# Transposing the quantised weight tiles by DMA instead of on TensorE, and leaving them byte-interleaved

## The reference

```python
agg_w = jnp.einsum('bk,koi->boi', att, weight[..., 0])
y = jnp.einsum('boi,bih->boh', agg_w, x) + agg_b[:, :, None]
def _bitlinear(x, w):
    scale = jnp.mean(jnp.abs(w))
    q = jnp.round(jnp.clip(w / (scale + EPS), -1.0, 1.0))
    return x @ (q * scale).T
gate, up = _bitlinear(y, w_gate), _bitlinear(y, w_up)      # w_gate, w_up: 2752 x 1024
return x + _bitlinear(gate * up, w_down)                    # w_down: 1024 x 2752
```

## Time and profile before

| | us |
|---|---|
| median of the runs | 1797.23 |
| the profiled execution | 1797.76 |
| its span, first to last instruction | 1796.0 |
| TensorE busy (with ends that are modelled) | 1738.4 |
| VectorE, ScalarE, GpSimd busy | 1118.9, 541.0, 141.4 |
| chunk 0's groups, from the first to the last matmul | 61.0 to 252 |
| chunk 0's downs | 260.2 to 334.7 |

### The profile page before, as it was taken

How to read it: one execution, slowest core, us unless ns; L and a number is a source line. 1 busy time by engine, 2 the same in 40 slices (tenths; PEclk the granted TensorE clock), 3 DMA queues, 4 the chain that set the end, 5 groups by cost and what they waited for, 6 DMA issues and landing times.

```text
span 1796.0 us, 29810 instructions
## 1 busy us (share of the span) xinstructions
PE 1738.4 (97%) x11897; PEld 1165.2 (65%) x11897; DVE 1118.9 (62%) x1831; ACT 541.0 (30%) x845; POOL 141.4 (8%) x96
## 2 busy tenths in 40 slices
PE   5698999999999999999999999999999999999999
PEld 3244454444545959678685968679594977768584
DVE  5989965686442545856467555855468455766464
ACT  4677441122211313323132312323132322333030
POOL 0854510010000000000000000000000000000000
PEclk9799999999999999999999999999999999999999
DMA  8437511243002312242113312141022412222021
GB/s 314 155 128 258 156 53 71 100 183 123 4 24 79 113 40 103 80 158 79 69 56 138 118 42 97 69 173 63 27 98 106 150 62 93 73 101 81 21 104 47
DMA packets 56557, 180.10 MB, mean 100 GB/s; under 512 B 6112, under 2 KB 6432, under 8 KB 56416
## 3 DMA queue, kind: packets, MB, share of 16 engines
q1 hardware_dynamic: 53712, 163.60, 26.1%
q0 software_dynamic: 2480, 14.22, 2.0%
q10 hardware_dynamic: 224, 0.28, 0.0%
HBM read 147.07 MB, written 31.01 MB: 99 GB/s over the span
## 4 chain that ended last, share of the span: by engine, by line
PE 90%; DVE 3%; issue 2%; ACT 1%; POOL 1%; DMA 1%; SPq 0%; DVEq 0%; POOLq 0%; ACTq 0%
PE ps L795 43%; PE ps L609 25%; PE ps L852 20%; PE ps L813 2%; DVE msk L1297 1%; ACT g_r L970 1%; DVE msk L1289 1%; POOL ys L577 1%; DMA bbc<-biasd 1%; PE ps L689 0%; ACT wgT L1005 0%; POOL ab L588 0%; POOL bbc L588 0%; DMA inter<-in_L_cond_b_dram 0%; DVE ys L1216 0%
## 5 line engine op out<-in xcount | busy, mean ns | idle before, releaser
L795 PE MATMUL ps<-yp,wgT 128*128 128x256 f16 x3528 | 773.4, 273 | 1.6 <-DVE xr L1346 1.0
L795 PE MATMUL ps<-wuT,wgT 128*128 128x256 f16 x3528 | 773.4, 273 | 0.0
L795 PEld LDWEIGHTS ps<-yp,wgT 128*128 128x128 fp8e4 x3528 | 345.3, 98 | 44.5 <-issue 3.5
L795 PEld LDWEIGHTS ps<-wuT,wgT 128*128 128x128 fp8e4 x3528 | 345.2, 98 | 41.4
L852 PE MATMUL ps<-wdT,inter 128*128 128x512 fp8e4 x1680 | 371.3, 379 | 0.0
L852 PEld LDWEIGHTS ps<-wdT,inter 128*128 128x128 f16 x1680 | 163.8, 98 | 194.7 <-issue 1.1
L1606 DVE SCALAR_TENSOR_TENSOR xr<-ps,osc,xr 128x512 f32<-128x512 f32 x180 | 134.1, 748 | 146.6 <-PE ps L852 111.5
L1555 DVE TENSOR_TENSOR wdT<-ps,msk 128x512 f32<-128x512 f32 (+1 forms) x66 | 44.0, 666 | 177.9 <-PE ps L795 177.9
L609 PE MATMUL ps<-yp,wgT 128*128 128x512 f16 x672 | 151.8, 384 | 2.9 <-DVE yp L1251 1.8
L609 PE MATMUL ps<-yp,wuT 128*128 128x512 f16 x672 | 152.8, 384 | 0.0
L609 PE MATMUL ps<-wdT,inter 128*128 128x512 fp8e4 x672 | 147.7, 379 | 0.0
(11 more groups left out here) (230 smaller groups left out, 1708.7 us busy)
## 6 DMA issues: line engine op xcount, KB each, us to landing
wgT<-wcomb SPq DMA_DIRECT2D x60, 896.0 KB, 4.7
wdT<-dcomb SPq DMA_DIRECT2D x12, 2240.0 KB, 10.6
xa<-in_x_dram SPq DMA_DIRECT2D x8, 2048.0 KB, 8.0
out_dram<-xr SPq DMA_DIRECT2D x64, 256.0 KB, 2.0
wdT<-in_L_ffn_w_up_dram SPq DMA_DIRECT2D x10, 512.0 KB, 4.7
wcomb<-raw POOLq DMA_DIRECT2D x11, 448.0 KB, 2.7
ys<-in_L_ffn_w_down_dram SPq DMA_DIRECT2D x9, 512.0 KB, 4.4
wcomb<-msk POOLq DMA_DIRECT2D x10, 448.0 KB, 2.7
```

Of the source, the lines that this page charges most:

```text
L795: last = nc.tensor.matmul(out, w, operand(i, OPERAND[what])[:, k, :], start=(start and h + k + i == 0), stop=(k == KQ - 1 and i == 1), ski ...
```

## The change

The four steps keep their places in `order0`, but the transposing is no longer an instruction of TensorE. SyncE issues a transposing DMA per tile, from `msk` (2-byte words, up to four blocks of 128x128) straight into the weight tensors, whose layout changes: the pairs of bytes stay pairs, so that a matmul reads its weights at a step of two bytes (`weight`, `down_weight`). Four semaphores `s_te`, one per `msk` buffer, tell that a tile has landed; TensorE waits for them ahead of a group, and VectorE before it quantises tile n + 4. `copy_T` and `identb` are gone, and so is GpSimd's part of the quantising: VectorE makes both instructions for all 68 tiles. The remainder of 704 columns is quantised in three pieces instead of two. All sums after the gate matrix's are on ScalarE (before, 15 of 46 were on VectorE). The opening is in another order: `agg_w(1, g)` after the norms, its copies on ScalarE, and other places for the first sums. In `combine` the three plain copies go to ScalarE (`copies`), and GpSimd's store waits for both engines.

```diff
-    SUM_DVE = (0, 1, 7, 10, 17, 21)
-    on_act = [i not in SUM_DVE if i < NG else i % 4 != 1 if i < 2 * NG else
-              i % 3 != 1 if i < 2 * NG + 12 else i % 2 == 0 for i in range(NQ)]
+    SUM_DVE = (0, 1, 7, 10, 17, 20)
+    on_act = [i not in SUM_DVE for i in range(NQ)]
...
-        wgT = sb("wgT", [P, KH, FT * P], f8)
...
-        wdT = sb("wdT", [P, FT + 1, H], f8)
+        wgT = sb("wgT", [P, FT, KH * P], f8)
...
+        wdT = sb("wdT", [P, (FT + 1) // 2, 2 * H], f8)
...
+        def weight(w, f, k):
+            return w[:, f, (k % KQ) * 2 * P:(k % KQ + 1) * 2 * P].rearrange("p (c i) -> p i c", i=2)[:, k // KQ, :]
...
+        def transposed(n):
+            if n < 2 * NG:
+                f = hidden(n)
+                if f < FT:
...
+            r, m = divmod(n - 2 * NG, DP)
+            count = -(-tiles[n][2] // (2 * P))
+            return wdT[:, m * KQ:m * KQ + count, :].bitcast(bf16)[:, :, r * P:(r + 1) * P]
+        def transpose_done(n):
+            return s_te[n % NM], 16 * (n // NM + 1)
...
+                last = buf[:, both:both + 2 * P].rearrange("p (c i) -> p i c", i=2)
+                parts.append((src[:, both:both + P], last[:, 0, :]))
+                parts.append((src[:, both + P:cols].unsqueeze(1).broadcast_to([rows, 2, FR]),
+                              last[:, 1, :].rearrange("p (z c) -> p z c", z=2)))
+            return parts
...
+            def transpose(n):
+                rows, cols = tiles[n][1:]
+                sp.wait_ge(s_q, n + 1)
+                width = -(-cols // (2 * P)) * 2 * P
+                sp.dma_start(transposed(n), msk[0:rows, n % NM, 0:width].bitcast(bf16),
+                             transpose=True).then_inc(s_te[n % NM], 16)
...
+                    while turned < NQ and (turned <= n0 if quant else place_s >= NG and
+                                           quant_at[turned] < order0.index(("S", place_s))):
+                        transpose(turned)
+                        turned += 1
...
-            for n in range(1, NQ, 2):
...
-                raw_arrived(pool, q_load[n])
...
-                nc.gpsimd.tensor_scalar(gts[n // 2 % 2][0:rows, 0:cols], raw(q_load[n]),
-                                        thr[0:rows, m:m + 1], None, ALU.is_gt).then_inc(s_gt, 1)
...
-            def transpose(n):
...
-                pe.wait_ge(s_q, n + 1)
-                if n >= 2:
-                    pe.wait_ge(s_te, n - 1)
...
-                buf = msk[0:rows, n % NM, :].bitcast(bf16)
...
-                    w = min(P, width - q)
-                    last = nc.tensor.transpose(bank[0:w, q:q + rows], buf[:, q:q + w], identb[0:rows, 0:rows])
-                last.then_inc(s_t, 1)
...
                 conv(0, k)
-                if k % 2:
-                    agg_w(1, k // 2)
             norms(0)
+            for g in range(OG):
+                agg_w(1, g)
             norms_T(0)
             total(0)
             for what, n in order0:
-                if what == "T" and n != 1:
-                    transpose(n)
-                elif what == "W":
...
                 elif what == "G":
-                    if n == 0:
-                        pe.wait_ge(s_te, 1)
...
-                    pe.wait_ge(s_te, NG + n + 1)
+                    if n == 0:
+                        pe.wait_ge(*transpose_done(FT))
+                    pe.wait_ge(*transpose_done(NG + n))
                     group(0, FT + n)
...
-            for k, n in enumerate((4, 5, 6, 8, 9, 11, 12, 13)):
+            for n in (4, 5, 6, 8, 9):
                 raw_sum(n)
+            for k, n in enumerate((11, 12, 13, 14, 15, 16, 18, 19)):
                 magnitudes(0, k)
-            for n, tiles_y in ((14, ()), (15, ()), (16, (0, 1)), (18, (2, 3)), (19, ()), (20, (4, 5, 6, 7))):
                 raw_sum(n)
-                for k in tiles_y:
-                    hi_y(0, k)
-            copy_T(0)
+            raw_sum(21)
+            for g in range(OG):
+                act.wait_ge(s_agg, OG + g + 1)
+                agg_copy(nc.scalar.copy, 1, g, s_agg1)
+            for k in range(KH):
+                hi_y(0, k)
...
+            def copies(i):
...
+                for b, a, r in ((0, 0, 0), (3, 0, 1), (6, 1, 1)):
+                    last = nc.scalar.copy(blocks7(i)[:, b, :, :], source(i, a, r), saturate=False)
+                last.then_inc(s_combA, 1)
...
-                if n % 2 == 0:
-                    raw_arrived(dve, e)
...
-                    last.then_inc(s_gtv, 1)
-                    dve.wait_ge(s_gtv, n // 2 + 1)
...
-                    if n >= NM:
...
+                if n >= NM:
+                    dve.wait_ge(*transpose_done(n - NM))
+                for src, dst in quantised(n):
+                    last = V.tensor_scalar(dst, src, thr[0:rows, m:m + 1], None, ALU.is_gt, saturate=False)
+                last.then_inc(s_gtv, 1)
+                dve.wait_ge(s_gtv, n + 1)
+                for src, dst in quantised(n):
+                    last = V.scalar_tensor_tensor(dst, src, nthr[0:rows, m:m + 1], dst, ALU.is_lt, ALU.subtract,
                                                   saturate=False)
...
-                if k in (2, 4, 6, 7):
-                    g = (k - 1) // 2
-                    dve.wait_ge(s_agg, OG + g + 1)
-                    agg_copy(1, g)
-                if k in (3, 5):
-                    raw_sum(7 if k == 3 else 10)
+            raw_sum(7)
+            raw_sum(10)
             scales(0)
             for k in range(SCD):
                 scale_y(0, k)
             raw_sum(17)
-            for k in range(4):
+            raw_sum(20)
+            partition_sums(0, NG)
+            for k in range(2):
                 split_y(0, k)
-            raw_sum(21)
-            partition_sums(0, NG)
...
-                for b, src in ((0, b11), (3, b21), (6, b22)):
-                    V.tensor_copy(st[:, b, :, :].bitcast(f16), src.bitcast(f16))
```

More of the change, by code:

```diff
@@ L145, in adaln_ternary_ffn @@
     assert nt == NQ and ns == NQ
+    ends = (NG, 2 * NG, NQ)
+    quant_at = {n: -1 for n in range(NM)}
+    for at, (what, n) in enumerate(order0):
+        if what == "T" and n + NM not in range(ends[min(n // NG, 2)], ends[min(n // NG, 2)] + NM):
+            quant_at[n + NM] = at
+        elif what == "W":
+            quant_at[n * NG] = at
+        elif what == "Q":
+            quant_at[n] = at
+    assert len(quant_at) == NQ
     ctx = ExitStack()
@@ L239, in adaln_ternary_ffn, with agg_copy @@
         attd = inter[:, 4:6, :].rearrange("p h (o b) -> p h o b", b=B // 2)
-        def agg_copy(h, g):
+        def agg_copy(copy, h, g, done):
             half = B // 4
@@ L246, in agg_copy @@
             for e in range(2):
-                nc.vector.tensor_copy(dst[e * C:(e + 1) * C, :, h * half:(h + 1) * half, g],
-                                      src[e * C:(e + 1) * C, :, :, e]).then_inc(s_aggv, 1)
+                copy(dst[e * C:(e + 1) * C, :, h * half:(h + 1) * half, g],
+                     src[e * C:(e + 1) * C, :, :, e]).then_inc(done, 1)
         def bias_row(c):
@@ L356, in adaln_ternary_ffn @@
         s_thr = sem("s_thr")
-        s_gt = sem("s_gt")
         s_gtv = sem("s_gtv")
         s_q = sem("s_q")
-        s_t = sem("s_t")
-        s_te = sem("s_te")
+        s_te = [sem(f"s_te{i}") for i in range(NM)]
         s_x = sem("s_x")
@@ L474, in _ @@
                 sp.dma_start(raw(e), tiles[n][0]).then_inc(s_raw[s], 16)
+            while turned < NQ and quant_at[turned] < order0.index(("U", UP - 3)):
+                transpose(turned)
+                turned += 1
             sp.wait_ge(s_xr, NT)
@@ L478, in _ @@
             load_x(1)
+            while turned < NQ:
+                transpose(turned)
+                turned += 1
             sp.wait_ge(s_q, NQ)
@@ L730, in down @@
                 elif isinstance(c, int) and c == 0:
-                    pe.wait_ge(s_te, NQ)
+                    for w in range(NQ - NM, NQ):
+                        pe.wait_ge(*transpose_done(w))
                 else:
@@ L812, in leftover @@
                 for w, x in ((FT, inter_r[:, rows]), (FT - 1, f_last[0][:, rows]), (FT - 1, f_last[1][:, rows])):
-                    last = nc.tensor.matmul(bank[:, :], x, wdT[:, w, cols], start=(start and w == FT), stop=True,
+                    last = nc.tensor.matmul(bank[:, :], x, down_weight(w, cols), start=(start and w == FT), stop=True,
                                             skip_group_check=True)
@@ L1066, in _ @@
                 hi_y(1, k)
+            def copies(i):
+                if i < 2:
+                    for w in range(NQ - NM, NQ):
+                        act.wait_ge(*transpose_done(w))
+                else:
+                    act.wait_ge(s_wst[i % 2], 16 * (i // 2))
+                for b, a, r in ((0, 0, 0), (3, 0, 1), (6, 1, 1)):
+                    last = nc.scalar.copy(blocks7(i)[:, b, :, :], source(i, a, r), saturate=False)
+                last.then_inc(s_combA, 1)
+            for i in range(DN - 1):
```

(4 more changed lines are left out.)

146 lines of the change are left out of this document (51 added, 95 removed).

## The result

The changed kernel takes 1809.43 us (median of 4 runs, 1807.32 to 1810.34); the kernel before, on the same chip, 1797.31 (1796.82 to 1797.75). The ratio is 1.0064, 95% interval 1.0052 to 1.0076: slower by 12.1 us. The forecast was 1792.

A forecast was written before the change was run, and what follows sets the result against it. Chunk 0 was taken as bound by TensorE's transposes alternating with VectorE's work. Gains of 9.6, then 13.2 us shrink to 7.7 and 4.5, and end at 5.1 off 1797.76: 1792.7, less 0.5 for the median, 1792; range 1784 to 1825.

The forecast's parts named there:

- Part 1: Quantising by VectorE alone: 1.98 us for each of 68 tiles; losing GpSimd's half costs and gives nothing.
- Part 2: Opening: first group ends near 66 instead of 67, worth 1 us (0 to 2); tile 1's quantising starts at 61.3.
- Parts 3 and 4: Chunk 0's gate groups, then up tiles: second threshold at 104.4, 9.6 us gained at tile 22; product 0 at 149.2, 13.2 gained.
- the unknown: The transposing DMA's price in chunk 0: landing taken as 4.4 us, free up to 5.5, so nothing added; 9.0 would add 37.
- rival B: Tiles 1 to 43: the four-buffer ring paces VectorE, or SyncE's issues exceed 1.98 us a tile; typically 1812, chance 0.26.
- Part 5: Product 0 to third threshold: ScalarE's row of sums takes 16.6 us, threshold at 166.0, gain left 7.7.
- Part 6: Product 4 to product 16 of chunk 0: VectorE bounds it, 56.7 us; product 16 at 229.0, gain shrinks to 4.5.
- Part 7: Product 16 to chunk 0's downs: 26.1 us, with waits for the next `x` and bias; downs at 255.1 instead of 260.2.
- Part 8: The rest after chunk 0's downs start: ScalarE's extra combine copies fit under 3.45 us a group, so nothing added.
- rival E: Weights read at a two-byte step slow TensorE's matmuls: 1800 to 1945, chance 0.05.
- C: Third threshold does not wait for ScalarE's row of sums and comes at 160.5, all after it 5.5 earlier: 1786, chance 0.11.
- D: No difference: waits for `x` and bias and the low clock after two idle stretches take 4 us more: 1797, chance 0.14.

The follow-up runs named there:

- e8: The kernel before, with VectorE making both comparisons of every tile and GpSimd none: 1795.61 us, ratio 0.9994.
- e1: The changed kernel, with transposes issued one ahead of each load of two eight-load bursts instead of behind them: 1802.26 us, ratio 1.0027.
- e2: The changed kernel, with six buffers of quantised tiles instead of four: 1802.29 us, ratio 1.0026.
- e7: The changed kernel, with plain copies of the same bytes instead of transposing DMAs, so weights are not transposed: 1809.73 us, ratio 1.0072.
- e5: e1 with chunk 1's load of `x` issued ahead of the last four transposes and the residual copies moved forward: 1796.66 us, ratio 0.9995.
- e10: e8 plus the changed kernel's opening and the combine copies on ScalarE, still without DMA transposes: 1794.57 us, ratio 0.9983.
- e6: e1 with every second of the last twelve sums on VectorE: 1802.61 us, ratio 1.0028.
- e11: e5 with six buffers of quantised tiles and every second of the last twelve sums on VectorE: 1795.85 us, ratio 0.9989.
- e12: The changed kernel, with the eight loads (4 MB) ahead of transpose 10 issued by ScalarE in its own queue: 1807.23 us, ratio 1.0056.
- e3: The changed kernel, with the loads from the 23rd on issued by GpSimd in a queue of their own: 1839.57 us, ratio 1.0238.

## Why the prediction was wrong

**Part 1 held.** Tiles follow each other in 1.98 to 1.99 us, the second instruction takes 1.29; e8 shows that taking GpSimd's half away costs nothing.

**Part 2 held.** Tile 1 from 60.08 (forecast 61.3).

**Parts 3 and 4 failed, by the unknown.** Second threshold at 112.2 instead of 104.4, tile 22 at 113.47 instead of 105.6, product 0 at 162.6 instead of 149.2: 13.4 us late, against 15.3 us of waits for two transposes. Without these waits (e1) the threshold comes at 108.4 and product 0 at 156.5. So of the 13.4 us, 6.1 are the waits and 7.3 are late sums, which the forecast had not at all: 4.0 at the threshold, and the rest up to product 0, 2.9 of it a wait for ScalarE behind a sum. Part 3 let the row of sums run through to 104.4 and never asked when SyncE can issue the loads that they need; in e1 and e2 the last four go out at 96 to 102 us. How much of this late issue any kernel with the transposes in SyncE's row must pay was not tested.

**The step that failed is that L, issue to landing, "is free up to 5.5 us" and then "I take 4.4, hence nothing".** The median was right (4.5 and 4.9 us for the gate and up tiles), but the ring of four does not run on the median: it stops at the longest landing. And that was to be read before. I took the loads' usual 4.4 us; the same answer of the kernel before, 50 to 262 us, has the burst in it (KB each, median us to landing):

```profile
ys<-in_L_ffn_w_up_dram SPq DMA_DIRECT2D x4, 512.0 KB, 9.9
prod<-in_L_ffn_w_up_dram SPq DMA_DIRECT2D x1, 512.0 KB, 12.3
```

In the changed kernel the last load of the burst landed at 95.6 and the transpose behind it at 96.2. A landing of 12.3 us less the 5.5 that four buffers cover gives a wait of 6.8 us; the transpose's issue also began 3.8 us after its tile was ready, where the forecast had 0.4 for the issue, which makes the 10.2 measured.

Nor did the forecast add up the engines' work. In 55 to 280 us the packets of the loads' queue took 68.2% of 225 us, 153 us; before it was 45.6%, 103. So a transpose adds 0.75 us of packet time on all 16 engines ((153 - 103) / 68), and a load takes 512 KB / 334 GB/s = 1.6: 2.3 us a tile, where VectorE needs 1.99. By e7's 58.7% a plain copy adds 0.43, so transposing as such 0.3 us. But this sum does not set the pace here. Where one load and one transpose go out for each tile of 1.99 us, the share is above 1, no tile waits, and loads and transposes issued in 62 to 78 us land in 4.8 to 5.0 and 4.6 us at the median:

```profile
68.00:78.00 10.00, 10.00 (x48) 4.49 (x46) 9.82 (x12) 7.29 (x13) 0.00 (x0) 1.00 1.09 316
```

In e1 that pace holds up to 97 us, with 0.3 us of waits. What stops VectorE is the burst on top of it.

Of the two prices that the Trainium skill gives, the runs lie by the second: by the 261 GB/s for transposing DMAs (DMA: Bandwidth & Descriptors, Latency and other measured facts) a tile takes 0.5 us, an estimate, and 0.75 of packet time was measured. By the 1309 ns a block (VectorE: DVE Perf Modes, The three transpose paths), taken as throughput, a tile would need 5.2, an estimate too; here one comes every 1.99 us without a wait. Neither would have told of the burst.

**SyncE's issues.** Taken at 0.4 us, a transpose's issue takes 1.20; with the load's 0.58 it fits in 1.99, by 0.2 us. The second half of rival B did not come about.

**Part 5 held:** 16.4 us from product 0 to the third threshold, for the reason given. The forecast's terms add up to 16.6, and its time 166.0 stands 16.8 behind product 0. **Part 6 held:** product 4 to 16 in 57.8 us (56.7). **Part 7 held:** 26.8 us to the downs (26.1). Its middle was also a place to gain: in e5 5.6 us come from the load of `x` being issued ahead of the last four transposes, with its copies moved forward. From product 0 to the downs the forecast was 1.0 us short in 107.

**Part 8 was wrong by 1.6 us, and its cause is open.** The copies are not it (e10). From the downs to the end the profiled executions took 1535.4 to 1535.8 us in the four kernels without the DMA transposes. With them it was 1537.0 to 1537.5 in six, 1539.1 and 1539.3 in e6 and e11, but only 1536.0 in e12 and 1536.2 in e3. Nearly all of it arises between chunks 3 and 6: from one chunk's first matmul of `wrT` to the next it takes 206.0, 206.1 and 205.8 us, before 205.5, 205.4 and 205.5; up to chunk 3 there is no difference except 0.3 us in e6 and e11. The one edit that reaches this loop is that the weights of the last 64 columns are read interleaved. A fixed price of that reading does not fit e12, where two of the three distances (205.8, 205.5, 205.5) are the old ones. The trace puts a part down to idle time of TensorE without a releaser (1.4 us against 0.3 to 0.7 in the kernels without the DMA, 0.8 in e12):

```profile
PE ps L830 <- issue: 1.4, 5, 0.4
```

**Interleaved weights** cost nothing where they are read: 9.23 us for 42 matmuls, rival E out.

**The rivals.** B was the one: a ring of four, stopped by late landings, "typically 1812". But it does not pace every tile, as B had it; it stopped VectorE twice. For B the text said that "in the crowded stretches a load lands late", against it the 4.4 us of a load; the first should have decided. C and D are out by the third threshold and the time.

## What to carry to other kernels

A ring of buffers that empties through DMA stops at the slowest landing, not at the median: look in the trace for the bursts among the other transfers in that stretch, and take the landing of the burst's last transfer as the new one's, and add the time for which its issue stands behind the burst's. Ask the same of every load that stands behind the new transfers in the issuing engine's row. Adding up packet time per step (here 2.3 us against 1.99) tells that the engines are near full, not that they set the pace. Against a burst, spreading the loads or lengthening the ring helps (7 us each, once); another queue does not. And where a change has independent parts, run them apart: this one had parts worth 2.9 us, hidden under others that cost 14.8.

## What the runs showed of the hardware

- Issuing a transposing DMA of 128x1024 bytes holds SyncE for 1.19 to 1.20 us where nothing backs up; a plain copy of the same tile 0.46, a 512 KB load behind it 0.58. In the burst four transposes took 11.6 us, four plain copies 2.6 (e7).
- Two hardware queues, SyncE's and ScalarE's, do not shield one another: a transpose landed in up to 15.0 us though the burst was in the other queue (e12).
- A share of the DMA engines above 1 can be sustained: 1.09 over 10 us with one 512 KB load and one transpose every 1.99 us, and no growing landing times.
- With the loads issued by GpSimd the engines moved 180 GB/s in 79 to 98 us at a share of 1.07 (the loads 2.91 MB, 153 GB/s), against 334 with all in SyncE's queue; the kernel took 30 us longer (e3).
